# A feature-crossing tower on one core: 26 filler matmuls where there were ten, and two loads of ScalarE issued later in the first tile

## The reference, cut to what matters

```python
x0 = xk = e                                   # 1024, 39, 16
for idx, (W, b) in enumerate([(w0, b0), (w1, b1), (w2, b2)]):
    z = relu(einsum('bhd,bkd,hks->bsd', x0, xk, W) + b)
    if idx != 2:
        xk = z[:, :64, :]                     # the first half goes on
        direct.append(z[:, 64:, :])
    else:
        direct.append(z)
z = sum(concatenate(direct, axis=1), axis=-1) # 1024, 256
h = concatenate([z, dense_ctx], axis=1)
h = maximum(h @ W_top1 + b_top1, 0)
h = maximum(h @ W_top2 + b_top2, 0)
y = h @ W_top3
```

## Time and profile before

| | us |
|---|---|
| median of 3 runs | 1269.59 (1266.67 to 1270.83) |
| the profiled execution, its own time | 1268.23 |
| its span, first to last instruction | 1266.4 |
| PE busy | 1231.7 (97%) |
| DVE busy | 1165.7 (92%) |
| POOL busy | 900.8 (71%) |
| ACT busy | 707.7 (56%) |

### The profile page before, as it was taken

The page is one execution under the profiler, slowest core; times in us unless marked ns, Lnnn a source line. Parts: engine busy times, 40 slices in busy tenths (PEclk is TensorE's granted clock), DMA queues, the critical chain, the costliest instruction groups (busy, mean ns, idle before and its releaser), DMA issues.

```text
span 1266.4 us, 15522 instructions
## 1 busy us (share of the span) xinstructions
PE 1231.7 (97%) x4256; PEld 783.5 (62%) x4256; DVE 1165.7 (92%) x1045; ACT 707.7 (56%) x741; POOL 900.8 (71%) x569
## 2 busy tenths in 40 slices
PE   4879999999999999999999999999999999999999
PEld 2446666666666666666666666666666666666664
DVE  7479999989999999999999999999999999999991
ACT  1245655556565655556655655557555565565552
POOL 7676777876878787787877778787878755654540
PEclk7789999999999999999999999999999999999999
DMA  7699878777998888888988888889888888897510
GB/s 210 151 167 222 202 180 187 180 196 191 219 213 178 185 190 197 201 200 210 215 178 185 192 193 201 203 210 219 177 181 195 194 200 198 206 219 174 134 51 0
DMA packets 135922, 234.42 MB, mean 185 GB/s; under 512 B 16403, under 2 KB 25101, under 8 KB 135787
## 3 DMA queue, kind: packets, MB, share of 16 engines
q1 hardware_dynamic: 84335, 151.67, 52.1%
q10 hardware_dynamic: 41994, 79.99, 24.8%
q0 software_dynamic: 9568, 2.47, 2.1%
HBM read 230.21 MB, written 6.23 MB: 187 GB/s over the span
## 4 chain that ended last, share of the span: by engine, by line
PE 83%; DMA 5%; DVE 4%; POOL 3%; SPq 2%; issue 2%; ACT 1%; DVEq 0%; ACTq 0%; POOLq 0%
PE z_odd L1041 33%; PE z_even L1041 31%; PE z_even L1075 7%; PE z_odd L1075 6%; DMA x_rep<-x_rows 2%; DVE whole L889 2%; DMA x_shift<-x_rows 2%; POOL rest L583 2%; PE whole_psum L1069 1%; DVE whole_psum L889 1%; PE x_odd L1095 1%; POOL gathered L568 1%; PE x_even L1095 1%; SPq L441 1%; DVE rest L906 1%
## 5 line engine op out<-in xcount | busy, mean ns | idle before, releaser
L583 POOL TENSOR_TENSOR rest<-whole,head 128x1024 fp32r<-128x1024 f32 x256 | 611.2, 2398 | 247.8 <-ACT head L701 247.2
L889 DVE TENSOR_TENSOR whole<-x_banks,x_rep 128x1024 f32<-128x1024 f32 x448 | 534.1, 1216 | 35.7 <-ACT x_banks L659 30.7
L701 ACT CAST head<-whole 128x1024 fp32r<-128x1024 f32 x256 | 268.6, 1049 | 159.0 <-DVE whole L889 120.7
L568 POOL DMA_INDIRECT gathered<-in_tbl,idx x299 | 286.7, 959 | 82.2 <-issue 74.1
L701 ACT CAST head<-whole_psum 128x1024 fp32r<-128x1024 f32 x192 | 194.8, 1015 | 142.0 <-DVE whole_psum L889 135.8
L889 DVE TENSOR_TENSOR whole_psum<-x_banks,x_rep 128x1024 f32<-128x1024 f32 x192 | 235.5, 1226 | 5.8 <-DMA x_rep<-x_rows 3.5
L906 DVE TENSOR_TENSOR rest<-whole_psum,head 128x1024 fp32r<-128x1024 f32 x192 | 234.5, 1222 | 0.3 <-ACT head L701 0.3
L1041 PE MATMUL z_odd<-head,w_rest 128*128 128x512 f32 x427 | 198.0, 464 | 3.9 <-POOL rest L583 3.3
L1041 PE MATMUL z_even<-head,w_rest 128*128 128x512 f32 x405 | 186.3, 460 | 1.0 <-DVE rest L906 0.8
L1041 PE MATMUL z_odd<-whole,w_whole 128*128 128x512 f32 x400 | 185.3, 592 | 0.5 <-DVE whole L889 0.5
L1041 PE MATMUL z_odd<-head,w_head 128*128 128x512 f32 x460 | 182.5, 397 | 0.0
(11 more groups left out here) (117 smaller groups left out, 1001.5 us busy)
## 6 DMA issues: line engine op xcount, KB each, us to landing
x_rep<-x_rows ACTq DMA_DIRECT2D x128, 512.0 KB, 11.7
x_rep<-x_rows SPq DMA_DIRECT2D x128, 512.0 KB, 11.7
x_shift<-x_rows SPq DMA_DIRECT2D x93, 546.0 KB
x_rep<-x_rows ACTq DMA_DIRECT2D x32, 384.0 KB
x_rep<-x_rows SPq DMA_DIRECT2D x32, 384.0 KB
x_rep<-x_rows SPq DMA_DIRECT2D x32, 256.0 KB
gathered<-in_tbl,idx POOLq DMA_INDIRECT x299, 7.0
x_rows<-xt_and_ctx SPq DMA_DIRECT2D x32, 78.0 KB
```

The lines of the kernel that those rows point to most:

```text
L568: nc.gpsimd.indirect_dma_start(gathered[:, f, :], None, tables[f], bass.IndirectOffsetOnAxis(ap=idx[:, f:f + 1], axis=0)).then_inc(s_gathe ...
L583: nc.gpsimd.tensor_tensor(rest[:, split_slot(product)], whole_slot(product), head[:, split_slot(product)].bitcast(F32), ALU.subtract).then ...
L701: nc.scalar.copy(head[:, split_slot(product)], src).then_inc(s_head, 1)
L889: nc.vector.tensor_tensor(out[0:rows, 0:width, :], xk[0:rows, :].unsqueeze(1).to_broadcast([rows, width, N]), x0, ALU.mult).then_inc(s_pro ...
```

## The change

Two edits. The number of filler matmuls behind the small tables' sums goes from 10 to 26. In the first tile's step ACT issues its halves of groups 0 and 1 of the next tile behind the heads of pairs 7 and 9 of layer 1, and no longer behind those of pairs 1 and 2. All other tiles keep pairs 1 and 2. SP's halves of the same groups stay where they are.

```diff
-WARM_UP = 10
+WARM_UP = 26
@@ act, body
-                    heads(t, 1, start=n, upto=n + 1, loads={1: [0], 2: [1]} if has_layer0(t) else {})
+                    early = {7: [0], 9: [1]} if is_first(t) else {1: [0], 2: [1]}
+                    heads(t, 1, start=n, upto=n + 1, loads=early if has_layer0(t) else {})
```

## The result

The changed kernel took 1272.54 us in the median of 8 runs (1271.48 to 1275.08). The kernel before took 1269.55 on the same chip (8 runs, 1266.67 to 1270.83). The ratio is 1.0030, with a 95% interval of 1.0018 to 1.0042. So it is slower by 0.3%, a small difference, but one that the interval tells from none. The forecast was 1263.5, faster by 0.5%, in a range of 1260.0 to 1269.5, and the result lies outside it. The profiled execution of the changed kernel took 1271.85 (span 1270.0).

The account below looks back on a forecast made before the run. PE, 97% busy, was taken as the bound, losing time in three opening waits and the low clock behind them. -3.0 - 3.26 + 0.4 + 0.5 = -5.4 us gave 1263.5 us, range 1260.0 to 1269.5.

Parts of the forecast that it names:

- the 26 run from 35.98 to 42.04 [...] the fillers cost the transposes 0.1 us: Opening: 26 fillers close PE's 3.67 us wait for `emb`, which ends at 41.98, delaying the transposes by only 0.1 us.
- I count 0 for the 5 us: Layer 1, pair 1: PE arrives 5 us sooner but still waits for POOL until 70.87; worth 0, bounds 0 and 5.
- worth nothing by itself: Earlier issue of `x_shift` of tile 1 gains nothing: DMA engines are full, and tile 0's groups precede it in SP's queue.
- even 3 us late, PE would not be missed there: Layer 1, pair 1: PE's wait for POOL, 3.07 us deep, would also hide a late PE.
- The slower rival: Opening: fillers run at the lower clock, transposes 5.5 us late, `x_shift` slips; +2.9 us, 1271.8; chance 0.07.
- the clock should not fall behind it: Opening, behind the filled hole: full clock from 42 to 54 for transposes, selects and first layer-0 pair, saving 5 us.
- The predicted saving of 5 us: Opening's transposes, selects and first layer-0 pair at full clock: at most 6 us saved, 5 taken.
- Part 2: Moving ACT's two loads later lets `x_shift` of tile 1 land 3.0 us sooner, at 84.7 where it was 87.7.
- The hole is 0.7 us where it was 3.7: Ahead of layer 0 of tile 1: PE's wait shrinks because `x_shift` lands sooner; -3.0 us.
- the -3.0 and the -3.26: Layer 0 of tile 1: 3.0 us from PE's shorter wait, 3.26 from 14 matmuls at full clock (9.43 to 6.17).
- what PE gains there reaches the end of the run: Behind 89.09, from layer 0 of tile 1: PE hardly waits again, so its gain there shortens the whole run.
- S: Follow-up theory: PE runs short of instructions in the sums, from the 16 added matmuls or, later, a place in its program.

Follow-up runs that it names:

- e12: The unchanged kernel before, profiled a third time; its one execution took 1268.12 us.
- e4: The unchanged kernel before, profiled a second time; its one execution took 1271.88 us.
- e3: The changed kernel with both edits, timed and profiled once more; 1273.81 us, ratio 1.0045 to the kernel before.
- e1: Kernel before with only the fillers behind the sums raised from 10 to 26, ACT's loads unmoved; 1274.42 us, ratio 1.0049.
- e6: Kernel before with no fillers behind the sums instead of 10, ACT's loads unmoved; 1269.30 us, ratio 0.9997.
- e2: Kernel before with only ACT's two loads moved behind pairs 7 and 9, ten fillers kept; 1270.67 us, ratio 1.0018.
- e10: Kernel before with ACT's two first-tile loads moved out of layer 1 into layer 2, behind pairs 2 and 4, ten fillers; 1274.32 us, ratio 1.0047.
- e5: Kernel before with 18 fillers behind the sums instead of 10 and ACT's loads behind pairs 7 and 9; 1270.27 us, ratio 1.0013.
- e11: Kernel before with 40 fillers ahead of the sums instead of 24, ten behind them, loads unmoved; 1269.94 us, ratio 1.0000.
- e9: Kernel before with 8 fillers ahead of the sums instead of 24 and none behind instead of 10; 1267.38 us, ratio 0.9991.
- e7: Kernel before with 8 fillers ahead of the sums instead of 24, all else unchanged; 1267.73 us, ratio 0.9989.

## Why the prediction was wrong

**The step that failed: "the 26 run from 35.98 to 42.04 [...] the fillers cost the transposes 0.1 us".** The length was right: 6.52 us against 6.06. The start was not. It was read from one execution whose sums ran through, and in 13 of 14 traces they end 8 to 9.5 us later. `emb` waits for the same sums but comes only 2 us behind them, so the room for fillers is about 2.2 us and not 6. Ten fill it (e12: no idle time), and 26 overrun it by 4.3 to 4.5. The 3.67 us hole was the room of an unusual execution. The holes themselves could not be seen in the one trace. What could be seen there is what held `emb`, in ACT's timeline:

```profile
38.64 1.54 ACT L655 CAST w_head<-whole 128x256 fp32r<-128x256 f32 x3
40.09 1.75 ACT L719 COPY emb<-gathered 128x1872 f32<-128x1872 f32 x1
```

and in e12:

```profile
44.50 1.75 ACT L719 COPY emb<-gathered 128x1872 f32<-128x1872 f32 x1 [3.18 <-DVE gathered L856]
```

In the first trace `emb` stood behind ACT's own casts of the weights, and not behind the sums, which had been ready for 4 us. In e12 it follows the sums, and ACT is idle 3.18 us ahead of it. So the room was ACT's casts, and sums that come later than these casts take it away. The prediction did not ask what happens if the sums come later.

**"I count 0 for the 5 us", for POOL holds that place: right in the profiled execution, and not in the other two with 26 fillers.** PE takes pair 1 at 74.78 in e12, 74.90 in e4 and 75.07 in the changed kernel. But e3 takes it at 82.96 and e1 at 79.50, since ACT's head came only at 79.41 and 75.94, behind POOL's last early gather. ACT had begun on the opening's layer 0 at 75.66 and 72.19, in e1 4.4 us behind PE's end of it, and what it waited for the profile doesn't name. Right, as far as the traces go, is that the issue of `x_shift` is "worth nothing by itself": e6 issued it 10 us later than e12 and had it 1.8 later. That it is tile 0's groups that set when it is served no run shows. But "even 3 us late, PE would not be missed there" looked at PE alone. The stores of `x_rows`, with which that stream begins, hang on the transposes directly and have no cover. The slower rival knew this; the sum of the forecast did not.

**"the clock should not fall behind it": wrong.** It was 0.53 in the changed kernel over the first layer-0 group (56.31 to 59.90), which took 3.63 us, and 0.50 in e3 for all of 56 to 72. The predicted saving of 5 us was a loss of 1.65 in that group against e12. By e6 a fall need not matter to the time. The prediction took it that the clock fell because of the hole. The trace of e3 has the fall without a hole. The Trainium skill (TensorE: Matmul & The Clock Gate, "Part 1") says that activity lifts the clock from its lower default. For the fillers the trace agrees: the granted clock is 0.50 in 41:45 and 0.90 in 45:51. Sixteen busy microseconds at 0.50 in e3 do not fit it.

**Part 2, "3.0 us" off the transfer: the mechanism is there, and the size about 1.8 us.** With 26 fillers DVE had `x_shift` 3.46 us sooner (e1 against the changed kernel; e3, the same kernel, had it 3.66 sooner still), with ten it made hardly a difference (e2 against e4 and e12), and with the loads out of the way entirely it was 4.7 us of the mean (43.1 against 38.4, e10). The traces of the kernel before differ among themselves by 3.3 (40.7 to 44.0). The Trainium skill (DMA: Bandwidth & Descriptors, "Queues, rings and completion order") lets the engines take turns between queues, which allowed 3.3 us. The mean lies below that bound; the turns themselves no row shows.

**"The hole is 0.7 us where it was 3.7": the hole is not the same in each execution.** The three traces of the kernel before have 3.75, 2.48 (e4) and none (e12). In e12 PE comes to layer 0 of tile 1 at 90.36 and at full clock (6.17 for the 14), because pair 1 came 4 us later than in the earlier trace rows and DVE only 1.1 later. There the -3.0 and the -3.26 had nothing to be taken from. Part 2 alone (e2) did come to 0.85 and 6.28, and gained nothing in the end. In the changed kernel the late transfer made a hole of 8.54 and a clock of 0.76 behind it, 8.15 for the 14.

**"what PE gains there reaches the end of the run": wrong.** Of 7.23 us between the changed kernel and e12 at tile 2, 3.72 were left at tile 7. e2 had its small hole and full clock, and was not ahead at tile 2. e6 was 5.5 late at tile 1 and lost nothing, and e10 was 1.9 early and ended slower.

**The rivals.** The slower one had the path right: fillers that end too late, stores of `x_rows` and `x_shift` that slip, PE's own part hidden at pair 1 (in the profiled execution). Its figures, transposes 5.5 late and +2.9 in all, are near the 4.47 and +3.0 found (1272.54 against 1269.55). Its cause was wrong. It wanted the lower clock in the fillers, which cost 0.5 here; the late sums did the rest. It had a chance of 0.07 because it hung on that cause alone.

**Open.** What tears the sums: the profile names no releaser, and S explains it neither by the added matmuls nor, for the end of the holes, by the place. One 16 KB packet on the instruction queue came at 33.3 in the trace without holes and at 41 to 42 in most others, but at 36.3 in the changed kernel and 34.2 in e5, so it isn't shown to be the cause. Also open are e2's 0.18%, what sets the clock in the opening, and why e3 kept its lateness and e6 did not.

## What to carry to other kernels

Before filling a hole, profile the unchanged kernel a second time and see whether the hole is there again. Here e4 alone would have shown that the fillers had no room. And ask of each hole what ends it: this one was as long as another engine's casts, and hung on sums that could come later. Filler work belongs ahead of the data that the path waits for, not between its arrival and its use: the same 16 matmuls were free ahead of the sums (e11) and cost half a per cent behind them (e1). A wait that covers an engine covers that engine alone, and not in every execution, so the transfers that start from the delayed step are to be followed by themselves.

## What the runs showed of the hardware

- In 13 of 14 traces PE ran one or a few instructions at a time, about 0.7, 1.4 or 2.1 us apart (0.20 busy, then 0.5, 1.2 or 1.9 idle in e12 and e6), for some ten us of the opening, with nothing that the profile could name ahead of them, 6 to 8 us in sum. 24 fillers ahead of the sums gave 12 to 14 matmuls before the first hole (21 in e5), 8 gave 29 or 30 (e9, e7), and with 40 the fillers themselves were hit (e11). In all of them it was over by about 41 us.
- The granted clock was 0.50 over 16 us of a wholly busy PE (e3, 56 to 72), behind ten us at 0.99 that were as busy, and 0.83 over 56 to 66 in another execution of the same kernel (windows).
- Three executions of the kernel before began layer 0 of tile 1 at 89.09, 90.36 and 91.70 and took 1268.23, 1268.12 and 1271.88. Positions near the start of a run say little of its end.
